# Attention and feed-forward layer: part of the softmax denominator added up by an accumulating DMA, feed-forward products taken later, and a reordered end

## The reference

```python
xn = layernorm(x)
q, k, v = heads(xn @ Wq.T), heads(xn @ Wk.T), heads(xn @ Wv.T)
diff_sq = max(|q|^2 + |k|^2 - 2 q.k, 0)
denom   = max((1 - |q|^2) * (1 - |k|^2), 1e-6)
distance = arccosh(max(1 + 2 * diff_sq / denom, 1))
attn = softmax(-distance) ; a = (attn @ v) @ Wo.T
ffn  = xn @ quantise_int4(kernel) + bias + (xn @ A) @ B      # rank of A, B is 16
out  = x + a + ffn
```

## Time and profile before

| | us |
|---|---|
| runs | 2315.15 (2313.09 to 2316.01), 3 runs |
| profiled execution, its own time | 2314.24 |
| its span (first to last instruction) | 2312.4 |
| PE busy | 2201.1 (95%) |
| DVE busy | 2083.9 (90%) |
| ACT busy | 2074.4 (90%) |
| POOL busy | 313.4 (14%) |
| chain that ended last | PE 56%, ACT 19%, issue 11%, DVE 10%, SPq 2%, DMA 2% |

### The profile page before, as it was taken

How to read it: one execution, slowest core, us unless ns; L and a number is a source line. 1 busy time by engine, 2 the same in 40 slices (tenths; PEclk the granted TensorE clock), 3 DMA queues, 4 the chain that set the end, 5 groups by cost and what they waited for, 6 DMA issues and landing times.

```text
span 2312.4 us, 45533 instructions
## 1 busy us (share of the span) xinstructions
PE 2201.1 (95%) x17416; PEld 863.7 (37%) x17416; DVE 2083.9 (90%) x2794; ACT 2074.4 (90%) x1909; POOL 313.4 (14%) x193
## 2 busy tenths in 40 slices
PE   6999999999999999999999999999999999988886
PEld 2443333334343434434334433343433444322222
DVE  7779898999999999999999999999999999888987
ACT  4379999999999999999999999999999999999992
POOL 0101111111111111111111111111111111100003
PEclk9999999999999999999999999999999999999998
DMA  4354332534545343455425354453344543344433
GB/s 145 118 146 114 100 108 68 154 112 134 145 137 140 104 131 109 142 140 143 133 86 151 105 151 131 125 158 101 116 126 146 136 141 110 87 119 103 123 96 96
DMA packets 355428, 285.04 MB, mean 123 GB/s; under 512 B 81132, under 2 KB 294252, under 8 KB 355208
## 3 DMA queue, kind: packets, MB, share of 16 engines
q1 hardware_dynamic: 355208, 282.10, 43.0%
HBM read 159.77 MB, written 121.36 MB: 122 GB/s over the span
## 4 chain that ended last, share of the span: by engine, by line
PE 56%; ACT 19%; issue 11%; DVE 10%; SPq 2%; DMA 2%; POOL 1%; ACTq 0%; DVEq 0%; POOLq 0%
PE pM L305 20%; PE pU L225 12%; PE pO L237 11%; ACT root L529 9%; ACT root L535 8%; PE pZ L253 6%; DVE root L871 3%; DVE root L866 2%; PE pM L295 2%; ACT qk L556 1%; SPq L1112 1%; PE pM L278 1%; PE pO L305 1%; DVE kx L739 1%; PE pM L281 1%
## 5 line engine op out<-in xcount | busy, mean ns | idle before, releaser
L529 ACT ACTIVATE root<-pU 128x1024 f32<-128x1024 f32 x1008 | 1016.9, 1039 | 78.2 <-PE pU L225 72.8
L535 ACT ACTIVATE root<-root 128x2048 f32<-128x2048 f32 x512 | 989.5, 1933 | 46.0 <-DVE root L866 46.0
L866 DVE TENSOR_SCALAR root<-root 128x2048 f32<-128x2048 f32 (+1 forms) x512 | 647.0, 1264 | 71.5 <-ACT root L529 71.2
L225 PE MATMUL pU<-QS,KS 100*128 100x512 f16 x2048 | 610.6, 381 | 40.9 <-ACT root L529 37.2
L871 DVE TENSOR_TENSOR root<-root 128x2048 f32<-128x2048 f32 x256 | 586.2, 2290 | 1.0 <-PE pO L237 0.9
L237 PE MATMUL pO<-root,VX 128*32 128x512 f32 x4096 | 505.8, 607 | 7.8 <-ACT root L535 7.7
L1018 POOL TENSOR_TENSOR sqr<-qk 128x512 f32<-128x512 f32 x112 | 208.5, 1862 | 997.0 <-ACT qk L556 910.9
L225 PEld LDWEIGHTS pU<-QS,KS 100*128 100x128 f16 x2048 | 175.2, 98 | 384.0 <-issue 143.4
L253 PE MATMUL pZ<-root,ones 128*32 128x512 f32 x2048 | 269.3, 597 | 18.3 <-DVE root L871 18.3
L237 PEld LDWEIGHTS pO<-root,VX 128*32 128x32 f32 x4096 | 103.9, 109 | 283.9 <-issue 191.4
L1013 POOL TENSOR_TENSOR xts<-xts,bias_b 128x512 f32<-128x512 f32 x64 | 82.9, 1297 | 680.2 <-PE pM L295 622.9
(11 more groups left out here) (228 smaller groups left out, 2210.3 us busy)
## 6 DMA issues: line engine op xcount, KB each, us to landing
v_d<-v_o SPq DMA_DIRECT2D x64, 264.0 KB, 2.1
k_d<-kx SPq DMA_DIRECT2D x64, 264.0 KB, 2.1
KT<-k_d SPq DMA_DIRECT2D x64, 264.0 KB
VX<-v_d SPq DMA_DIRECT2D x64, 264.0 KB
xts<-in_x SPq DMA_DIRECT2D x32, 512.0 KB, 4.3
res_d<-f_o SPq DMA_DIRECT2D x64, 256.0 KB, 3.9
QS<-qh_d SPq DMA_DIRECT2D x128, 128.0 KB
KS<-kh_d SPq DMA_DIRECT2D x128, 128.0 KB
```

The source lines that it names most:

```text
L225: mm = pe.matmul(pU[:, col:col + HALF], KS[i][:, h, j * P:(j + 1) * P], QS[i][:, h, half * HALF:(half + 1) * HALF], start=True, stop=True)
L529: act.activation(root[:, q % RING, cols], pU[:, cols], ACT.Square).then_inc(squared, 1)
L535: act.activation(root[:, q % RING, :], root[:, q % RING, :], ACT.Sqrt).then_inc(rooted, 1)
L866: v.tensor_scalar(root[:, q % RING, cols], root[:, q % RING, cols], CS * CS, CS * CS, ALU.max, ALU.subtract).then_inc(clamped, 1)
```

## The change

- **Denominator.** In periods 8 to 55 (`HELD`) the pair sum of key tiles 0 and 1 is written by VectorE into a buffer of its own, `held`. The pair sum of tiles 2 and 3 is added to it by a DMA that GpSimd issues with an add (`accumulate`, 128x2048 f32, 1 MiB). TensorE does nothing at k = 11 and 15; at k = 3 of the next period it multiplies `held` and the pair of tiles 4 and 5 by ones, at k = 7 the last pair. The seven slots become four for even and three for odd tiles (`slot`, `wait_free`). Even tiles' slot of j = 2 is free only when the DMA has landed.
- **Feed-forward.** The split, transposed x of each tile is stored (`store_xT`, `xT_d`) and loaded again seven periods later (`load_feed`, with x itself). Tile m's product (`feed`) runs in period m + 7, for tiles 49 to 55 in periods 56 to 62; tiles 56 to 63 have theirs at k = 0 to 2 of periods 56 to 63. The prologue and periods 0 to 6 have none. Quantising, folding and splitting the matrix move from the prologue into periods 0 to 4, that of Wo to periods 4 to 6. `load_res` goes: `take_o` reads `xr`, where `take_f` left its result.
- **Division.** One tile in every period instead of two in every even one.
- **Prologue.** Fixed PSUM banks in place of a rotation.
- **End.** `divide(56)` becomes `divide_pair`, after the last `add_pair`; `load_three` is issued by GpSimd, and no longer waits in SP's queue behind `pass_kv`.

Core of the diff ("..." marks what is left out):

```diff
+        HELD = range(LEAD, LATE)
+        def slot(q):
+            return 4 + q // 2 % 3 if q % 2 else q // 2 % 4
+        def wait_free(engine, q):
+            u = q - 6 if q % 2 else q - 8
+            if u < 0:
+                return
+            p, j = u // JC, u % JC
+            if j % 2:
+                engine.wait_ge(pair_added, u // 2 + 1)
+                engine.wait_ge(v_summed, u + 1)
+            elif p not in HELD or j >= 4:
+                engine.wait_ge(summed_up, u + 2)
+            elif j == 0:
+                engine.wait_ge(pair_added, u // 2 + 1)
+            else:
+                engine.wait_ge(accumulated, 16 * (p - HELD[0] + 1))
...
             def sum_one(q):
+                first = j == (JC - 3 if p in HELD else 1)
+                if p in HELD and j < JC - 3:
+                    return
...
+                if p in HELD and first:
+                    pe.wait_ge(accumulated, 16 * (p - HELD[0] + 1))
+                    for h in range(G4):
+                        pe.matmul(pZ[h * HD:(h + 1) * HD, :], ones[:, :], held[:, h * HALF:(h + 1) * HALF], start=True, stop=False)
...
             def add_pair(q):
...
+                if q // JC in HELD and q % JC == 1:
+                    v.wait_ge(summed_up, q // JC * JC)
+                    into = held[:, :]
...
+            def accumulate(p):
+                q = p * JC + 3
+                g.wait_ge(pair_added, q // 2 + 1)
+                g.dma_start(held[:, :], root[:, slot(q - 1), :], accum_op=ALU.add).then_inc(accumulated, 16)
...
             for n in range(LEAD, NT):
                 square_qk(n, 0)
                 square_qk(n, 1)
...
+                if n >= LEAD + F_LAG:
+                    g.wait_ge(featT_made[0], n + 1)
+                    add_bias(n - LEAD - F_LAG)
+                if n - LEAD in HELD:
+                    accumulate(n - LEAD)
...
             for n in range(LEAD):
...
+                    pe.wait_ge(taken["q"], n)
+                    project(n, "q", 0, 0, 12)
+                    pe.wait_ge(taken["k"], n)
+                project(n, "k", 1, 0, 12)
+                transpose_x(n + 1, 5)
...
+                project(n, "v", 4, 0, 12)
...
-                    project(n - 1, "f", (u + 2) % 4, 0, 12)
...
+                elif k in (0, 1, 2):
+                    feed(p, 0, 4 * k, 4 * k + 4)
...
+                if p == 0:
+                    if k == 3:
+                        largest_of("f", 5, "raw")
+                    elif k == 10:
+                        quantise(0)
...
-                    if even and k == 3:
+                    if k == 3:
                         divide(o)
...
             add_pair(QUADS - 3)
             clamp(QUADS - 1)
-            divide(56)
             add_pair(QUADS - 1)
+            divide_pair()
             divide_last()
...
             def divide_two():
                 g.wait_ge(raw2_loaded, 5 * 16)
                 g.wait_ge(made["k"], NT)
+                g.wait_ge(pair_divided, 1)
```

More of the change, by code:

```diff
@@ L312, in project, with feed, low_rank_rows @@
                     mm.then_inc(made[k], 1)
+            def feed(m, b, first, last):
+                late = m >= NT - LEAD
+                t = xT[m % 2] if late else fT[m % 2]
+                if first == 0 and late:
+                    pe.wait_ge(fT_late[m % 2], ((m - NT + LEAD) // 2 + 1) * 16)
+                elif first == 0:
+                    pe.wait_ge(fT_loaded[m % 2], (m // 2 + 1) * 16)
+                if m == 0 and first == 0:
+                    pe.wait_ge(w_low, 4)
+                mm = product(pM[b], lambda c: t[:, 0, c, :], lambda c: t[:, 1, c, :], W["f"], first, last)
+                if last == 3 * KC:
+                    mm.then_inc(made["f"], 1)
+            def low_rank_rows(c, b):
+                if c == 0:
+                    pe.wait_ge(rank_loaded, 2 * 16)
+                pe.matmul(pM[b][:, :], At[:, c * P:(c + 1) * P], Bl, start=True, stop=True).then_inc(low_rank, 1)
             def output(o, b, first, last):
-                cols = slice(o % 2 * P, (o % 2 + 1) * P)
-                mm = product(pM[b], lambda c: ah[:, c, cols], lambda c: al[:, c, cols], W["o"], first, last)
+                mm = product(pM[b], lambda c: ah[:, c, :], lambda c: al[:, c, :], W["o"], first, last)
                 if last == 3 * KC:
@@ L1024, in ratio, with load_three @@
                 return g.tensor_tensor(lo, of, hi, ALU.subtract)
+            def load_three():
+                blk, groups = NB - 1, KC - 1
+                rows = rz_d[blk * H:blk * H + groups * G4, :]
+                g.wait_ge(xn_done, NT)
+                g.wait_ge(feat_stored, NT // 2 * 64)
+                g.wait_ge(att_stored, 32 * (PERIODS - 2))
+                g.dma_start(raw3, att_d[blk * DM:blk * DM + groups * P, :].rearrange("(g p) n -> p g n", p=P)).then_inc(raw3_loaded, 16)
+                g.wait_ge(divisors, NB - 1)
+                g.dma_start(rows.rearrange("r (q n) -> (r q) n", q=P // H), zc[0:P - P // KC, 1, :]).then_inc(rz3_stored, 16)
+                g.wait_ge(rz3_stored, 16)
+                for h in range(G4):
+                    src = rows.rearrange("(g h) n -> h g n", h=G4)[h:h + 1].to_broadcast([HD, groups, BLK])
+                    g.dma_start(rzb3[h * HD:(h + 1) * HD, :, :], src).then_inc(raw3_loaded, 16)
             def divide_three():
@@ L1044, in gpsimd_program @@
             everywhere(scale[:, 2:3], 2, largest["v"])
-            everywhere(top[:, 6:7], 5, largest["f"])
-            everywhere(scale[:, 4:5], 4, summed_w["f"])
-            g.wait_ge(bias_loaded, 16)
-            for n in range(LEAD):
-                add_bias(n)
             for n in range(LEAD, NT):
@@ new lines, in load_feed @@
+            def load_feed(m):
+                rows, i = slice(m * P, (m + 1) * P), m % 2
+                if m < NT - LEAD:
+                    there = min(m + F_LAG + LEAD + 1, NT)
+                    for parity in range(2):
+                        sy.wait_ge(xT_stored[parity], (there + 1 - parity) // 2 * 16)
+                    if m >= 2:
+                        sy.wait_ge(made["f"], f_place[m - 2] + 1)
+                    sy.dma_start(fT[i][:, :, :, :].rearrange("p s c n -> p (s c n)"), xT_d[rows, :]).then_inc(fT_loaded[i], 16)
+                    if m >= 2:
+                        sy.wait_ge(taken["o"], m - 1)
+                        sy.wait_ge(f_stored, f_place[m - 2] * 16 + 16)
+                    sy.dma_start(xr[:, i, :], x[rows, :]).then_inc(xr_loaded[i], 16)
+                else:
+                    for parity in range(2):
+                        sy.wait_ge(xT_stored[parity], NT // 2 * 16)
+                    sy.wait_ge(made["v"], NT)
+                    if m >= NT - LEAD + 2:
+                        sy.wait_ge(made["f"], f_place[m - 2] + 1)
+                    sy.dma_start(xT[i][:, :, :, :].rearrange("p s c n -> p (s c n)"), xT_d[rows, :]).then_inc(fT_late[i], 16)
+                    sy.wait_ge(xT_made, NT)
+                    sy.wait_ge(summed, 2 * NT)
+                    if m >= NT - LEAD + 2:
+                        sy.wait_ge(featT_made[0], NT)
+                        sy.wait_ge(featT_made[1], NT)
+                        sy.wait_ge(k_stored, NT * 16)
+                        sy.wait_ge(v_stored, NT * 16)
+                    if m >= NT - LEAD + 2:
+                        sy.wait_ge(xb_done, f_place[m - 2] + 1)
+                    sy.dma_start(res_last[m - NT + LEAD], x[rows, :]).then_inc(xr_late[i], 16)
```

541 lines of the change are left out of this document (284 added, 257 removed).

## The result

The changed kernel takes 2301.0 us (median of 8 runs, 2298.2 to 2308.5) against 2314.5 (2311.2 to 2316.9, 8 runs) on the same chip: a ratio of 0.9948 [0.9933, 0.9963], 0.52% faster. The forecast was 2262, 2.3% faster. The profiled execution took 2301.53 us, its span is 2299.7 against 2312.4, its mean granted clock 0.986 against 0.989.

The account below looks back on a forecast made before the run. TensorE was taken as full in the middle and prologue, ScalarE as busiest in the tail. Terms -34 + 11 - 33 + 7 - 4 = -53 from the profiled 2314.2 gave 2261, as a median 2262 us; range 2240 to 2328.

Parts of the forecast that it names:

- Denominator, periods 8 to 55: Middle periods: dropping one of four sum_one calls saves TensorE 41 us, GpSimd's issue slows VectorE by 8; net 33 off.
- the accumulate's deadline: Middle periods: the adding DMA has about 9.9 us before anyone waits; landing taken as 9.3, so it just fits.
- if that cover were gone: Middle periods, SP's queue: added loads and stores cost nothing, being far ahead of use; otherwise late KV or fT loads.
- the 41 us of saved products: Periods 8 to 55: one sum_one call of 0.86 us fewer on TensorE in each of 48 periods.
- Rival 1: Middle periods: the accumulate lands late, each microsecond beyond about 9.9 costing 48; 2382 us if landing at 12.4; chance 0.20.
- Rival 2: Middle periods: GpSimd's issue holds up VectorE like its arithmetic, 2.9 us per period, giving 2327 us; chance 0.05.
- Rival 3: Middle not shortened: ScalarE and VectorE waits set the period, or slight lateness eats the gain; 2295 us; chance 0.15.
- Prologue: Before period 0: eight products go, then a loop of waits takes 10.15 us per tile; 34 us off, bounds 23 and 37.
- Periods 0 to 7: Early periods receive moved quantising, folding and splitting passes, which show in the time; 11 us added, bounds 0 and 13.7.
- the row of 37.87 us: Early period with Wo's share, 5.3 us longer than 32.6, read as evidence that added passes there do show.
- Tail: Periods 56 to 62: added products bring TensorE, ScalarE and VectorE close together at the present period; 7 us added.
- end: After the last period: removing a 5.5 us wait for GpSimd's division, moving 5.8 behind the last addition; 4 us off.

## Why the prediction was wrong

The direction held and the time lies in the range; the size is wrong, chiefly by one step.

**The step that failed** is "Denominator, periods 8 to 55", and in it not the sentences on the accumulate's deadline but those on everybody else: "The data lies far ahead of its use, and the engines' 43% leave room: nothing." A share of 43% is an average. The accumulate is issued when the feature stores and the KV rows are, and it delays them: at the new batches SP goes on 3.6 to 5.6 us later than in the kernel before. The last feature store stands at the head of a chain with no slack (store, wait, ten issues, load, product). The condition was written down ("if that cover were gone, it would show as a late KV or fT load"), but no price stood beside it, and VX and the stack loads, which SP waits to issue, were not on the list. Price: 35.2 us of traffic, 26.8 of it at the six boundaries, where leaving the accumulate out gave 31.9 back. Not all of period 55's stall is traffic: without any accumulate its interval is still 37.9 us against 31.7 before, with TensorE waiting 3.6 us for the first late load of x. That load, too, was costed at nothing.

**In the same step** the 41 us of saved products were real work saved but only 6.8 of time. In even periods the KV rows decide when TensorE may finish; they wait in SP's queue behind the five new loads, costed at nothing. Moved ahead of them, the loads gave 16.4 us in the middle, and the kernel without the boundary accumulates came to 2250.

**Also in it** the division per tile, "now 2 us every period: nothing", gave 20 us in the kernel before. By the sum, without this gain, which I had not foreseen, the kernel would have come out slower: that the direction held is luck. So is it that the ordinary pairs, 66.9 us, came near their forecast: the kernel without any accumulate has 66.95 in most of its pairs.

**The accumulate's cost to itself** was right: I took 9.3 us, it lands in 7.0 to 9.8, and 10.1 us of waits came of it. Rival 1 did not happen. The Trainium skill (DMA: Bandwidth & Descriptors, the anatomy of a DMA on the GpSimd path) gives 4.4 us by its fit, an estimate; measured is 8.2, and none of the 48 landed before 7.0. The same page (queues, rings and completion order) says that a DMA engine takes turns between the queues that have work for it, packet by packet. The store of 9.25 us fits that; that the 1 MiB costs each transfer beside it should have had a chance of its own among the rivals.

**Rival 2** fell: beside each of the 48 issues of 0.96 us VectorE does a clamp over 128x2048, and each of these 48 clamps takes its 1.22 us. **Rival 3**, the middle not shortened, comes nearest to what happened, with a time of 2295 and a chance of 0.15. Its first mechanism, VectorE and ScalarE at their floor, was not the one: in the run with odd accumulates most of these periods took the full 0.86. Its second, a little lateness of the accumulate, came to 10.1 us of waits.

**Prologue** -33.8 against -34: right. The splits of x come 10.2 and 10.8 us apart in turn, 10.5 on the average, forecast 10.15; a first q product "near 105" came at 106.16.

**Periods 0 to 7**: +3.0 against +11. A pass in periods 3 and 4 does show, as was read from the row of 37.87 us. But that row was a poor measure: of Wo's three passes only ScalarE's of 2.08 us lies in it, and the granted clock was 0.91 there and 1.00 in the intervals beside it. The maximum and the three passes of quantising measured 2.29, 1.29, 1.22 and 1.28 us, 6.1 together instead of 9.1. They lie ahead of period 0's copy, a stretch that grew by 4.8 us. When Wo's passes left periods 1 to 3, the interval of 37.87 us fell by 5.6 us, to 32.24.

**Tail** +11.6 against +7, **end** -11.6 against -4: together 0 against +3. The mechanism given, several engines at one limit, fits the five intervals, +5.9, but is not shown. Missed was that GpSimd's division would move from the end into the tail. Its term of the end, 5.5 removed, was right; "moving 5.8" behind the last addition cost nothing that the run without it shows. The other 6 us of the end were not foreseen. VectorE's clamp and addition, 6.2 us longer beside GpSimd's division in the kernel before, may be their cause; no run tests it.

The sum of the errors: 0.2 - 8.0 + 51.1 + 4.6 - 7.6 = 40.3, against a forecast of -53 and -12.7 measured. One figure of the range does not follow from its terms: with the middle at its upper bound the gain grows by 15 us, or by 23 without the 8 for VectorE, and not by 19.

## What to carry to other kernels

Before adding a large DMA, list the transfers issued within its 8 to 10 us and follow each to the first wait that has no slack; the mean DMA share says nothing about them, and a batch or block boundary is where such a wait stands. Work taken off a full engine counts only up to the next thing that it waits for: look for what arrives last, here small transfers behind others in one issue queue, and move those first. A cheap test is to add the traffic alone, then drop the new DMA where it collides: here leaving out six of 48 gave back 29 us.

## What the runs showed of the hardware

A DMA of 1 MiB from SBUF to SBUF that adds to its destination took 0.957 us of GpSimd to issue and landed after 7.0 to 9.8 us, median 8.2; 48 of them and GpSimd's few other DMAs took 11.0% of the 16 DMA engines over the span, 0.3% without them. A plain load of 1 MiB landed in 6.2.

The last feature store at a boundary, 256 KB, landed in 5.5 to 9.2 us beside it, and in 3.3 to 4.9 in the kernel that has no accumulate there. The issues of SP's queue are drawn out as well: the three groups of four small DMAs took 2.73, 2.49 and 4.78 us to issue, in the same place of the kernel without any accumulate 2.51, 3.33 and 2.49. Over all some 95 such groups the mean is 3.25 us with the accumulates and 2.70 without.

VectorE's subtraction of two tiles in SBUF took 0.69 us alone (one column of bias beside it) and 1.38 on average with GpSimd adding the bias at the time. The Trainium skill (SBUF — State Buffer, who interferes with whom) says that such a two-input instruction shares its second input's path with GpSimd's reads. The fall from 1.38 to 0.69 us, when GpSimd's addition was cut to one column, agrees.
